# Attention kernel: the order of TensorE's steps and the use of the PSUM banks changed

## The reference

```python
x = x + attn(layernorm(x)); x = x + ffn(layernorm(x))
def attn(x):                       # 16 heads of 16
    x_h = split_heads(x)
    xw = einsum('bhtd,hde->bhte', x_h, w_att_val)
    att = softmax(einsum('bhte,bhse->bhts', xw, x_h) / sqrt(16))
    vx = split_heads(x @ wv_w.T + wv_b)
    return merge_heads(einsum('bhts,bhsd->bhtd', att, vx)) @ out_w.T + out_b
```

## Time and profile before

| | us |
|---|---|
| median of 3 runs | 1658.5 |
| lowest and highest | 1653.16, 1659.29 |
| the profiled execution | 1653.08 |
| its span | 1651.3 |

### The profile page before, as it was taken

The page is one execution under the profiler, slowest core; times in us unless marked ns, Lnnn a source line. Parts: engine busy times, 40 slices in busy tenths (PEclk is TensorE's granted clock), DMA queues, the critical chain, the costliest instruction groups (busy, mean ns, idle before and its releaser), DMA issues. The chain is left out here.

```text
span 1651.3 us, 33543 instructions
## 1 busy us (share of the span) xinstructions
PE 1533.3 (93%) x8874; PEld 866.6 (52%) x8874; DVE 1340.0 (81%) x2731; ACT 852.9 (52%) x1714; POOL 525.0 (32%) x676
## 2 busy tenths in 40 slices
PE   3389999999999999999999999869999999999998
PEld 3134544544544544544544544336666766666666
DVE  7487787787787787787787777369999999999996
ACT  2156666666666666666666666623333333333332
POOL 2214314314314314314314312023444333444332
PEclk8589999999999999999999999989999999999999
DMA  4524344344344344344344333000000000000000
GB/s 161 155 73 124 105 116 117 104 115 117 104 115 117 104 116 117 104 116 117 104 115 117 104 104 124 11 1 14 16 16 16 16 16 13 16 16 16 16 16 19
DMA packets 82531, 127.34 MB, mean 77 GB/s; under 512 B 28864, under 2 KB 48448, under 8 KB 82368
## 3 DMA queue, kind: packets, MB, share of 16 engines
q1 hardware_dynamic: 74720, 119.55, 25.5%
q10 hardware_dynamic: 7776, 7.36, 1.4%
HBM read 81.67 MB, written 45.15 MB: 77 GB/s over the span
## 5 line engine op out<-in xcount | busy, mean ns | idle before, releaser
L1002 DVE TENSOR_REDUCE neg_max<-max_bank 128x1 f32<-128x512 f32 x1024 | 666.9, 683 | 189.8 <-PE max_bank L804 180.2
L941 ACT ACTIVATE probs<-scores 128x512 f32<-128x512 f32 x1024 | 555.8, 595 | 351.0 <-PE scores L818 347.3
L1343 PE MATMUL gu_bank<-splits,f_x_T 128*128 128x352 f32 x1024 | 315.6, 461 | 2.1 <-ACT f_x_T L1321 2.1
L815 PE MATMUL scores<-q_stack,x_stack 64*128 64x512 f32 x1024 | 256.1, 497 | 21.3 <-ACT probs L941 21.1
L830 PE MATMUL pv<-probs,v_quad 128*32 128x512 f32 x2048 | 272.7, 605 | 1.2 <-ACT probs L941 1.2
L815 PEld LDWEIGHTS scores<-q_stack,x_stack 64*128 64x128 f32 x1024 | 95.8, 183 | 299.3 <-ACT probs L941 269.2
L1343 PEld LDWEIGHTS gu_bank<-splits,f_x_T 128*128 128x128 f32 x1024 | 190.6, 191 | 98.4 <-ACT f_x_T L1321 2.7
L804 PE MATMUL max_bank<-x_stack,q_stack 64*128 64x512 f32 x1024 | 209.9, 406 | 27.1 <-DMA x_stack<-x_split 15.0
L818 PE MATMUL scores<-max_stack,max_ones 64*128 64x512 f32 x1024 | 203.3, 393 | 0.0
L1171 POOL TENSOR_TENSOR f_rstd<-f_mean_var,eps 128x1 f32<-128x1 f32 x64 | 44.7, 699 | 382.6 <-DVE f_mean_var L1281 382.6
L1361 PE MATMUL y_bank<-splits,h_T 128*128 128x256 f32 x640 | 148.9, 380 | 1.1 <-ACT h_T L1301 1.1
(11 more groups left out here) (128 smaller groups left out, 2004.9 us busy)
## 6 DMA issues: line engine op xcount, KB each, us to landing
q_stack<-q_split SPq DMA_DIRECT2D x512, 64.0 KB, 2.4
x_stack<-x_split SPq DMA_DIRECT2D x256, 128.0 KB, 2.7
x_split<-splits SPq DMA_DIRECT2D x64, 256.0 KB, 2.2
q_split<-splits SPq DMA_DIRECT2D x64, 256.0 KB, 2.3
out_dram<-x_all SPq DMA_DIRECT2D x64, 128.0 KB, 1.7
x_all<-in_L_attn_x_dram ACTq DMA_DIRECT2D x14, 512.0 KB, 5.0
max_rows<-max_turned SPq DMA_DIRECT2D x256, 4.0 KB, 1.8
max_stack<-max_rows SPq DMA_DIRECT2D x128, 8.0 KB
```

Of the source, the lines that this page charges most:

```text
L815: pe.matmul(scores[banks[m][0]][:, :], row_tile(x_stack[g], m)[:, p, j * P:(j + 1) * P], row_tile(q_stack[g], m)[:, p, :], start=True, sto ...
L941: act.activation(probs[j % 2][:, h, :], scores[bank_of(g, QUAD * j + h)[0]][:, :], ACT.Exp).then_inc(p_ready, 1)
L1002: dve.tensor_reduce(neg_max[g % 2][:, at:at + 1], max_bank[bank_of(g, k)[0]][:, :], AX.X, ALU.max, negate=True).then_inc(m_used, 1)
L1343: m = pe.matmul(gu_bank[c][:, :], x_T[u][:, a, :], gate_up_T[:, a, c * CH:(c + 1) * CH], start=(a == 0), stop=(a == HALVES - 1))
```

## The change

Each step now has one run of row-tile pairs: a max pair, both key-score pairs with their maxima, a max pair. Behind it stands either, in even steps, the values' matmuls of two key tiles at once, or, in odd steps, all the 128-row work, up to three pieces. The key tiles 0 and 1 are weighed in step (g,2), the tiles 2 and 3 in step (g+1,0), that is in the next quad, each half into a PSUM tile of its own. ScalarE copies the halves (`begin_half`, `end_half`), GpSimd adds them (`add_halves`). `probs` has four buffers in place of two, `scores` four banks in place of three. The other four banks are a ring: max scores, halves and pieces take the next bank in the order of the list `TILES_IN_RING`, which two empty places close, and `room` makes TensorE wait until the tile four places earlier is emptied. GpSimd's work is placed by a table, `POOL_STEP`; the statistics on VectorE move with it, and VectorE's pieces stand at a step's end. SyncE's order is not changed.

```diff
-    IN_STEP = {(0, 0): "x0", (0, 1): "q0", (0, 2): "rows3", (0, 3): "turn0",
-               (1, 0): "turn1", (1, 1): "proj0", (1, 2): "rows0", (1, 3): "proj1",
-               (2, 0): "x1", (2, 1): "q1", (2, 2): "rows1", (2, 3): "v0",
-               (3, 0): "v1", (3, 2): "rows2"}
-    ALL = list(IN_STEP.values())
+    IN_STEP = {(0, 1): ("x0",), (0, 3): ("rows3", "q0"), (1, 1): ("turn0", "rows0"), (1, 3): ("turn1",),
+               (2, 1): ("proj0", "x1"), (2, 3): ("q1", "v0", "rows1"), (3, 1): ("proj1",), (3, 3): ("rows2", "v1")}
+    ALL = [kind for kinds in IN_STEP.values() for kind in kinds]
     PREPARE = ("x0", "q0", "x1", "q1", "v0", "v1")
     FINISH = ("rows3", "turn0", "turn1", "proj0", "proj1")
+    BY_ACT = [kind for kind in ALL if kind[0] in "xq" or kind[:4] == "turn"]
+    BY_DVE = [kind for kind in ALL if kind not in BY_ACT]
+    TILES_IN_RING = []
+    for g in range(QUADS):
+        for j in range(TT):
+            TILES_IN_RING += [("max", g, QUAD * j + k) for k in range(QUAD)]
+            if j % 2 == 0:
+                TILES_IN_RING.append(("pv", g, j // 2))
+            else:
+                TILES_IN_RING += IN_STEP[g, j]
+    TILES_IN_RING += [None] * (-len(TILES_IN_RING) % len(ring))
+    AT = {tile: n for n, tile in enumerate(TILES_IN_RING) if tile}
...
-    STATS = [(0, 3), (1, 0), (1, 1), (1, 2)]
-    AGGREGATE = (1, 3)
+    STATS = [(0, 1), (1, 0), (1, 2), (2, 0)]
+    AGGREGATE = (2, 1)
+    POOL_STEP = {(0, 0): ("values",), (0, 1): ("halves", "x0"), (0, 3): ("q0",),
+                 (1, 0): ("values",), (1, 1): ("halves",),
+                 (2, 0): ("values",), (2, 1): ("halves", "x1"), (2, 2): ("deviation",), (2, 3): ("q1",),
+                 (3, 0): ("normal0", "values"), (3, 1): ("halves", "normal1"), (3, 2): ("normal2",),
+                 (3, 3): ("normal3",)}
...
+            def add_halves(i, g):
+                pool.wait_ge(pv_begun, i + 1)
+                pool.wait_ge(pv_ended, i + 1)
+                pool.tensor_tensor(pv_rows[g % 2][:, :], pv_more[:, :], pv_rows[g % 2][:, :], ALU.add)\
+                    .then_inc(pv_summed, 1)
...
-                for g in range(3):
-                    quad(b, g, first)
-                if prepared(b + 1):
-                    split("x0", b)
-                quad(b, 3, first)
-                if prepared(b + 1):
-                    split("q0", b)
-                if prepared(b + 2):
-                    deviation(b + 2)
-                if prepared(b + 1):
-                    split("x1", b)
-                    split("q1", b)
-                if prepared(b + 2):
-                    normalize(b + 2)
+                for g in range(QUADS):
+                    for j in range(TT):
+                        for task in POOL_STEP.get((g, j), ()):
+                            if task == "values":
+                                ready_values(b, g, first)
+                            elif task == "halves":
+                                if not (first and g == 0):
+                                    add_halves(QUADS * b + g - 1, (g - 1) % QUADS)
...
+            def weigh_values(b, g, second):
+                i, q = (QUADS * b + g - 1, (g - 1) % QUADS) if second else (QUADS * b + g, g)
+                tile = ("pv", g, 0 if second else 1)
+                steps = (2, 3) if second else (0, 1)
+                for semaphore, count in room([tile], b):
+                    pe.wait_ge(semaphore, count)
+                if not second:
                     pe.wait_ge(v_spread, i + 1)
-                    if not start:
-                        pe.wait_ge(pv_saved, i)
-                for k in range(QUAD):
-                    h = head_of(k)
-                    m = pe.matmul(pv[VW * h:VW * h + VW, :], v[g][:, j, h, :], probs[j % 2][:, k, :],
-                                  start=(j == 0), stop=(j == TT - 1))
+                for j in steps:
+                    pe.wait_ge(p_ready, QUAD * (TT * i + j + 1))
+                    for k in range(QUAD):
+                        h = head_of(k)
+                        m = pe.matmul(bank(tile)[VW * h:VW * h + VW, :], v[q][:, j, h, :], probs[j][:, k, :],
+                                      start=(j == steps[0]), stop=(j == steps[1]))
...
+                    if ahead:
+                        max_scores(b, g, PAIRS * j)
                     if j == 0:
                         pe.wait_ge(max_loaded[g], 16 * ROWS * (b + 1))
                     for p in range(PAIRS):
                         key_scores(i, g, j, p, start)
-                        if ahead:
-                            max_scores(i + 2, ab, ag, PAIRS * j + p, False)
-                        if p == 0 and j > 0:
-                            weigh_values(i, b, g, j - 1, start)
-                        elif p == 0 and not start:
-                            weigh_values(i - 1, b - (g == 0), (g - 1) % QUADS, TT - 1, False)
-                    if stands(kind, b):
-                        for half in range(2):
-                            other(half, kind, b)
+                    if ahead:
+                        max_scores(b, g, PAIRS * j + 1)
+                    if j == 0 and not start:
+                        weigh_values(b, g, True)
+                    if j == 2:
+                        weigh_values(b, g, False)
+                    for kind in IN_STEP.get((g, j), ()):
...
+            def end_half(i, g):
+                act.wait_ge(pv_done, 2 * i + 2)
+                wait(act, pv_summed, i)
+                act.activation(pv_more[:, :], bank(("pv", (g + 1) % QUADS, 0))[:, :], ACT.Copy).then_inc(pv_ended, 1)
+            def begin_half(i, g):
+                act.wait_ge(pv_done, 2 * i + 1)
+                act.activation(pv_rows[g % 2][:, :], bank(("pv", g, 1))[:, :], ACT.Copy).then_inc(pv_begun, 1)
...
+            def keep_values(kind, c):
                 a = int(kind[1])
                 dve.wait_ge(misc_ready, use(kind, c - 1) + 1)
                 wait(dve, v_spread, QUADS * c)
-                dve.tensor_tensor(v_dense[:, 2 * a:2 * a + 2, :], misc[:, :].rearrange("p (s e) -> p s e", e=E),
+                dve.tensor_tensor(v_dense[:, 2 * a:2 * a + 2, :], bank(kind)[:, :].rearrange("p (s e) -> p s e", e=E),
                                   v_bias[:, :].unsqueeze(1).broadcast_to([P, 2, E]), ALU.add)\
-                   .then_inc(misc_used, 1)
...
```

More of the change, by code:

```diff
@@ L528, in attention_block @@
     recip = sb("recip", [P, TT, QUAD])
[L530 to L533, removed]
+    scores = [pb(f"scores{k}", [P, T]) for k in range(QUAD)]
+    ring = [pb(f"ring{k}", [P, T]) for k in range(4)]
     stack_loaded = [sem(f"stack_loaded{g}") for g in range(QUADS)]
@@ new lines, in room @@
+    def room(tiles, b):
+        counts, sample = {}, {}
+        for tile in tiles:
+            n, c, probe = AT[tile], b, b if isinstance(b, int) else 2
+            while True:
+                n -= len(ring)
+                if n < 0:
+                    n, c, probe = n + len(TILES_IN_RING), c - 1, probe - 1
+                if isinstance(b, int) and c < -1:
+                    break
+                if in_ring(TILES_IN_RING[n], c):
+                    semaphore, count = emptied(TILES_IN_RING[n], c)
+                    size = emptied(TILES_IN_RING[n], probe)[1]
+                    if semaphore not in counts or size > sample[semaphore]:
+                        counts[semaphore], sample[semaphore] = count, size
+                    break
+        return list(counts.items())
@@ L717, in _ @@
             batch(B - 1)
+            add_halves(LAST, QUADS - 1)
         @block.sync
@@ L810, in key_scores @@
-                banks = [bank_of(g, k) for k in at]
-                free = [k - bank[1] + 1 for k, bank in zip(at, banks) if not (start and k < 3)]
-                if free:
-                    pe.wait_ge(p_ready, QUAD * TT * i + max(free))
+                if not (start and j == 0):
+                    pe.wait_ge(p_ready, QUAD * (TT * i + j - 1) + ROWS * p + ROWS)
                 for m in range(ROWS):
-                    pe.matmul(scores[banks[m][0]][:, :], row_tile(x_stack[g], m)[:, p, j * P:(j + 1) * P],
+                    pe.matmul(scores[ROWS * p + m][:, :], row_tile(x_stack[g], m)[:, p, j * P:(j + 1) * P],
@@ L861, in prepare @@
[L861 to L878 removed]
+                    pe.wait_ge(x_low, HALVES * c)
@@ L882, in other @@
-                    for s in range(2 * half, 2 * half + 2):
-                        m = pe.transpose(misc[:, s * P:(s + 1) * P], o_rows[:, s, a * P:(a + 1) * P],
+                    if a == 0:
+                        pe.wait_ge(sum_used, uses_before(b, BY_DVE))
+                    else:
+                        pe.wait_ge(sum_used, use("rows3", b, BY_DVE) + 1)
+                    for s in range(TT):
+                        m = pe.transpose(out[:, s * P:(s + 1) * P], o_rows[:, s, a * P:(a + 1) * P],
@@ L884, in other @@
                                          ident[:, :])
                 else:
[L886 to L891 removed]
```

(17 more changed lines are left out.)

297 lines of the change are left out of this document (148 added, 149 removed).

## The result

The changed kernel takes 1743.6 us (median of 4 runs, 1742.5 to 1744.6) against 1658.2 of the kernel before on the same chip: ratio 1.052, 95% interval 1.050 to 1.054, +85 us. Forecast was +2.3%, 1697 us. The direction is right and the time lies inside the range, but the move is more than twice as large as forecast.

A forecast was written before the change was run, and what follows sets the result against it. TensorE's order of work was taken as the bound, busy 59.90 of 61.93 us per batch. Without late arrivals 57.1, plus 4.3 and 4.3, gave 65.7; over all batches and ends +43.8 on 1653.1 us: 1697 us, range 1650 to 1745.

The forecast's parts named there:

- What the change removes: TensorE per batch: runs -3.1 us, values' groups -1.1, adjoining 128-row pieces -0.5, waits of 2.4 gone; own work becomes 54.8.
- what it adds at once: Per batch: ScalarE copies of 2.4 us beside idle time, GpSimd additions 4 x 1.28 mostly hidden, TensorE ring waits 2.3.
- ring waits: TensorE's waits for PSUM banks still in use, mainly after short pieces and at the list's end: 2.3 us per batch.
- The price of a change of tile shape: At the two ends of a TensorE run of row-tile pairs: 0.20 us; 16 fewer runs per batch give -3.1.
- the two waits don't show: Rival for the attention loop: neither late arrival costs time, 57.1 us per batch, 1568 us in all; chance 0.07.
- Late arrival one: At (2,0), scores wait for maxima from the later q0 through SyncE's queue: start at 30.05 not 25.75, +4.3 us per batch.
- Late arrival two: At (3,0), v0 waits for GpSimd to spread quad 3's values, holding TensorE's second max pair: +4.3 us per batch.
- 4 us or more: Sign of a right forecast: in each batch one max-pair wait this long behind VectorE's v0, itself waiting on GpSimd.
- The sum: Attention loop: 57.1 + 4.3 + 4.3 = 65.7 us per batch against 61.93; +43.8 us in total, 1697 us.
- The clock: Rival: idle waits lower TensorE's clock, 1.86 us a fall; 1725 us with one per batch, 1753 with two; chance 0.15.
- a granted clock under 0.97 in the loop: Sign named in advance as pointing to the rival of TensorE's lower clock in the attention loop.
- decisive is whether a gap of some 4 us is enough: Test for the lower-clock rival: whether loop waits this long lower TensorE's clock; loop waits of 0.62 us left it at 1.00.

The follow-up runs named there:

- e10: The changed kernel with q0 one step earlier, the fourth quad's values one quad earlier and the x_stack loads before the wait for q_split's store: 1582.8 us, ratio 0.9553.
- e7: The changed kernel with q0 and the fourth quad's values earlier, plus the step's second max pair put between a weighing's two key tiles: 1703.0 us.
- e2: The changed kernel with only q0's product moved one step earlier, from behind step (0,3) to behind (0,2): 1696.2 us, ratio 1.0235.
- e11: The changed kernel with only the four x_stack loads issued before SyncE waits for the store of q_split: 1701.6 us, ratio 1.0262.
- e1: The changed kernel with only the fourth quad's values spread one quad earlier, at quad 2's start: 1676.1 us, ratio 1.0113.
- e4: The changed kernel with 23 max pairs per batch computed again in front of the two waits, at (2,0) and (3,0), no arrival moved: 1687.9 us.
- e12: The kernel before the change, with the x_stack loads issued before the wait for q_split's store: 1659.6 us, ratio 1.0006.

## Why the prediction was wrong in its size

*What the change removes; what it adds at once.* Right. The forecast had 57.1 us a batch without late arrivals (1.60 a run, 1.85 a group, ring waits of 2.3); e10 has 57.4. Its waits for a bank of the ring from 256 to 1014 us are 10.4 (v_dense) and 12.3 (neg_max) in 13.2 batches, 1.7 each, so TensorE's own work is nearer to 55.7 than to the forecast's 54.8: two errors of less than a microsecond that cancel in part. The step lengths that the prediction lists sum to 56.75 and not to 57.1; nothing hangs on the difference. The price of a change of tile shape, 0.20, showed again: a run of six pairs takes 1.58 where two of three took 1.80, and e7 has 0.23. The rival "the two waits don't show", 1568, is what e10 comes to within 1%.

*Late arrival one.* Mechanism right: max_stack's issue at 27.4 us after the batch's start, scores at 29.72 for 30.05. The wait is 1.1 us for the stacks and 2.4 for the maxima (12.8 and 26.8 in 11 batches), 3.6 for the 4.3 of the forecast. e2 and e11, which shorten the same chain at different links, both leave 1.3 to 1.6 us of the wait and take 3.4 us out of the period.

*Late arrival two.* Mechanism right: v0 waits 5.45 us for GpSimd, the second max pair starts at 51.71 for 51.25. The wait itself is 3.4 for 4.3, under the "4 us or more" that the prediction named as its sign; the pair came to it later, since the lower clock had already held up step (2,0). e1 removes the wait by moving one quad's values. Together the two cost 7.1 us a batch, 8.6 was forecast.

*The sum.* The term that failed is the clock: entered with nothing in the sum, it measured 3.8 us a batch (e4). The period is 57.4 + 7.1 + 3.8 = 68.3 (the last two terms are differences of periods, so they close by themselves), where the forecast had 57.1 + 8.6 = 65.7. Late arrivals 1.5 us too dear hid part of the missing term; that is luck. The excess of 2.6 makes 34 us in the 13 batches of the loop, of 47 in all. The profiles before and after (spans 1651.3 and 1742.7) place the rest, if each batch is marked by ScalarE's copy of the weighed values in its first step: up to batch 1 the change loses 8.4 us (forecast 1.6), in batch 14 3.5 (2.3), between the last batch and feed-forward 1.6 (a gain of 1 was forecast), and in feed-forward 4.1 (0). The last batch gains 8.4, as forecast (8.5). The lower clock is in the first of these too (0.50 from 119.0 to 123.5 us, where the kernel before has 1.00). The 4.1 in feed-forward is not the change's: e12, with the loop of the kernel before, has 3.9 there.

*The rivals.* "The clock" was there, with its place, and with two falls it gave 1753 for the 1743.6 measured; it got 0.15. The prediction's own sign for it, a granted clock under 0.97 in the loop, came true with 0.93. The step that failed is the weighing: "decisive is whether a gap of some 4 us is enough". I had one row of an idle stretch of 7 us and waits of 0.6, nothing in between, and took the gap's size as speaking against a fall, although nothing in the trace did. A price per spell was read off well enough: 1.86, measured 1.4 at (2,0), and 1.7 + 0.5 = 2.2 at (3,0) and just behind. The Trainium skill, "TensorE: Matmul & The Clock Gate", section "Why this matters for your kernels", had said that idle gaps between bursts bring the lower clock; the runs agree for the long gaps: with the waits of some 2.5 and 3.4 us the clock is 0.93, with one of them 0.96 or 0.95, with 1.3 us left 0.99, with none or with work in them 1.00. Gaps of 0.8 us (e7) left it at 1.00.

## What to carry to other kernels

When an edit moves a producer later, follow its chain to the last landing, and if TensorE then waits for some us in a loop, price the spell at the lower clock behind the wait too: here half as much again as the waits (3.8 on 7.1). Matmuls added in the wait show within one run how much of a loss is clock. Moving the late link (a quad's values on GpSimd, q0 by one step, four loads ahead of a store's landing) turned the same change from +5.2% to -4.5%. A reorder of loads was worth nothing where nobody waits for them (e12), so look for it after the change and not before.

## What was not expected of the hardware

Merging transfers can cost far more than it saves: with 2 entries in the slowest dimension the DMA share during the loads was 0.13, about 2 of 16 engines, and the kernel took 2493 us for 1627; with 16 entries they spread again, but one issue on SyncE took 0.70 us in place of 0.49, so that 8 were as long as 12. And the lower clock came after waits of 2.3 to 2.6 us at (2,0), each with a wait of 1.1 us and one pair of matmuls just ahead of it, while seven waits of 0.8 us per batch (e7) left it at 1.00.
